# Four-layer sequence model on one core: shared expert mixtures for chunks 2 and 3 (latent) and for chunks 0 and 1 (distance), and new written orders for every engine

## The reference, cut to what matters

```python
# L0 (stage B): gates from the top two logits with a jitter mask, experts of width 256
h = silu(x @ w_gate[e].T) * (x @ w_up[e].T);  out += dense_w[:, e:e+1] * (h @ w_down[e].T)
# L1 "latent" (stage D2): softmax router, top 2, width 128, and one expert shared by all tokens
rw = softmax(nx @ Wr.T + expert_bias); topw, topi = top_k(rw, 2); topw = softmax(topw)
moe_out = swiglu(nx, sW1, sW2, sW3) + sum over the two experts of topw * swiglu_e(nx)
# L3 "distance" (stage H): the two nearest centroids, weights from a softmax over the two
#   distances, experts of width 342 with biases, gated by silu
```

## Time and profile before

| | us |
|---|---|
| runs | 1157.9, 1161.93, 1163.76 (median 1161.93) |
| profiled execution | 1159.38 |
| its span, first to last instruction | 1157.4 |
| PE busy | 920.3 |
| DVE busy | 727.3 |
| ACT busy | 609.2, of it 171.9 in 134 table loads |
| POOL busy | 403.8 |

### The profile page before, as it was taken

How to read it: one execution, slowest core, us unless ns; L and a number is a source line. 1 busy time by engine, 2 the same in 40 slices (tenths; PEclk the granted TensorE clock), 3 DMA queues, 4 the chain that set the end, 5 groups by cost and what they waited for, 6 DMA issues and landing times.

```text
span 1157.4 us, 19160 instructions
## 1 busy us (share of the span) xinstructions
PE 920.3 (80%) x5985; PEld 646.6 (56%) x5996; DVE 727.3 (63%) x2359; ACT 609.2 (53%) x1168; POOL 403.8 (35%) x443
## 2 busy tenths in 40 slices
PE   0286677995868877999958989999999989897791
PEld 0176656784647734654635645444446657687681
DVE  7684346383564776367658587876686766675442
ACT  0033255575435647687557644856567745544240
POOL 2435263535563662323324221430202203405413
PEclk9988789997869878999979999999999999988885
DMA  8246555644224103100132000000023435547771
GB/s 304 83 141 200 158 157 171 192 121 131 79 67 112 33 21 87 50 19 8 52 98 60 23 17 1 1 1 1 27 88 96 126 104 158 157 133 233 221 214 42
DMA packets 134516, 115.48 MB, mean 100 GB/s; under 512 B 11401, under 2 KB 130193, under 8 KB 134129
## 3 DMA queue, kind: packets, MB, share of 16 engines
q1 hardware_dynamic: 124704, 95.24, 28.3%
q0 software_dynamic: 6144, 12.60, 3.7%
q10 hardware_dynamic: 3568, 6.43, 1.6%
HBM read 95.08 MB, written 21.11 MB: 100 GB/s over the span
## 4 chain that ended last, share of the span: by engine, by line
PE 52%; ACT 14%; DVE 12%; issue 7%; another core or an unknown queue 5%; DMA 4%; POOL 4%; SPq 1%; POOLq 0%; ACTq 0%; DVEq 0%
PE bank L979 10%; PE bank L655 10%; PE bank L1002 5%; PE bank L597 5%; ACT L2098 5%; PE bank L701 4%; PE bank L740 2%; PE bank L604 2%; DMA att<-in_stage 2%; ACT att L2187 2%; PE bank L969 1%; PE bank L670 1%; PE bank L760 1%; PE bank L586 1%
## 5 line engine op out<-in xcount | busy, mean ns | idle before, releaser
L655 PE MATMUL bank<-xt_group,w_gu 128*128 128x128 f32 (+1 forms) x1440 | 210.2, 294 | 19.9 <-ACT hid L2136 5.7
L655 PEld LDWEIGHTS bank<-xt_group,w_gu 128*128 128x128 f32 (+1 forms) x1440 | 189.2, 200 | 36.1 <-issue 12.1
L2098 ACT ACT_TABLE_LOAD x134 | 171.9, 1283 | 36.6 <-PE bank L1002 17.2
L979 PE MATMUL bank<-picked,w_dyn 128*128 128x512 f32 x320 | 147.5, 612 | 0.7 <-DVE picked L1860 0.7
L701 PE MATMUL bank<-w_dn,hid 128*128 128x128 f32 (+1 forms) x720 | 115.2, 296 | 23.8 <-DVE hid L1493 16.8
L701 PEld LDWEIGHTS bank<-w_dn,hid 128*128 128x128 f32 (+1 forms) x720 | 99.9, 206 | 34.7 <-DVE hid L1493 19.7
L2540 POOL TENSOR_SCALAR rstd<-mv 128x4 f32<-128x4 f32 x32 | 6.6, 206 | 317.0 <-DVE mv L1305 316.3
L979 PEld LDWEIGHTS bank<-picked,w_dyn 128*128 128x128 f32 x320 | 60.5, 196 | 77.4 <-issue 75.7
L2580 POOL DMA_INDIRECT x_slots<-x,pos x64 | 62.8, 982 | 101.1 <-DVE pos L1445 84.3
L2660 POOL TENSOR_TENSOR att<-att,lsm 128x512 f32<-128x512 f32 x64 | 67.4, 1068 | 88.0 <-DVE lsm L1725 63.9
L2136 ACT ACTIVATE hid<-bank,early 114x128 f32<-114x128 f32 x180 | 52.7, 366 | 62.2 <-PE bank L655 40.6
(11 more groups left out here) (342 smaller groups left out, 1844.3 us busy)
## 6 DMA issues: line engine op xcount, KB each, us to landing
w_gu<-in_ffn SPq DMA_DIRECT2D x60, 342.0 KB
w_gu<-in_ffn SPq DMA_DIRECT2D x60, 256.0 KB
x_group<-x_slots SPq DMA_DIRECT2D x60, 192.0 KB
y_slots<-early SPq DMA_DIRECT2D x60, 192.0 KB
w_dn<-in_ffn SPq DMA_DIRECT2D x60, 192.0 KB
w_dn<-in_ffn SPq DMA_DIRECT2D x60, 128.0 KB
w_gu<-in_ffn SPq DMA_DIRECT2D x60, 128.0 KB
w_dn<-in_ffn SPq DMA_DIRECT2D x60, 64.0 KB
```

What stands on the lines that cost most here:

```text
L655: last = nc.tensor.matmul(bk[0:rows, o:o + 128], w_gate_up(k, st, j, half, f), xt_group[:, group_slot(k, st, g), c:c + 128], start=True, s ...
L979: last = nc.tensor.matmul(bk[:], part("dyn", "ex_w2")[:, h * 384 + at:h * 384 + at + 128], picked[:, 2 * h + t - 1, :], start=False, stop= ...
L2098: A.preload_act_table_set(name)
```

## The change

**Shared mixtures.** `SHARERS` puts chunks 2 and 3 into one D2 mixture and chunks 0 and 1 into one H mixture. The later chunk is the carrier: its blocks hold both chunks' assignments, 2048/128 + 7 = 23 blocks in 8 groups (seven of 3 and one of 2), where the two mixtures had 2 x 15 blocks in 2 x 5 groups. All of B, D2 of chunks 0 and 1, and H of chunks 2 and 3 stay alone with 15. The other chunk (2 in D2, 0 in H) has no turns, units, loads or stores of its own; it routes, scatters into the carrier's slots, waits for the carrier's last stores, gathers and combines.

**Counts.** Each sharer's counts wait for both chunks' one-hots and add the partner's totals: 1 more f32 matmul of 8 columns for the carrier, 5 for the other. `place` compares against 8 limits instead of 4. `name_blocks` works on 23 blocks and waits for the partner's counts; the biases are built in parts of at most 16 blocks.

**Set-up.** The slot arrays have 1 + 23 x 128 rows in place of 1 + 15 x 128, and the copies that fill `x_slots` grow with them. `stats` has two rotating rows in place of one per chunk.

The diff, cut:

```diff
-NB, GROUP = 15, 3
-GROUPS = NB // GROUP
-SLOTS = NB * 128
+GROUP = 3
+SHARERS = {"B": ((0,), (1,), (2,), (3,)), "D2": ((0,), (1,), (2, 3)), "H": ((0, 1), (2,), (3,))}
+def sharers(k, st):
+    return next(set_ for set_ in SHARERS[st] if k in set_)
+def carrier(k, st):
+    return sharers(k, st)[-1]
+def n_blocks(k, st):
+    return 8 * len(sharers(k, st)) + 7
+def n_groups(k, st):
+    return -(-n_blocks(k, st) // GROUP)
+MOST = max(n_blocks(set_[-1], st) for st in SHARERS for set_ in SHARERS[st])
+SLOTS = MOST * 128
...
-    "mix": ((0, "B"), (1, "B"), (2, "B"), (3, "B"), (0, "D2"), (1, "D2"), (2, "D2"), (3, "D2"), (0, "H"), (1, "H"),
-            (2, "H"), (3, "H")),
+    "mix": ((0, "B"), (1, "B"), (2, "B"), (3, "B"), (0, "D2"), (1, "D2"), (3, "D2"), (1, "H"), (2, "H"), (3, "H")),
...
@@ counts (PE)
-                pe.wait_ge(T.placed.s, T.placed.at(k, st, "counted"))
+                for q in sharers(k, st):
+                    pe.wait_ge(S[q].placed.s, S[q].placed.at(q, st, "counted"))
                 nc.tensor.matmul(bk[:, 0:40], part("const", "ones"), routing(s)[:, 40:80], start=True, stop=False)
+                for q in sharers(k, st):
+                    if q != k:
+                        for c in range(0, 40 if q > k else 8, 8):
+                            nc.tensor.matmul(bk[:, c:c + 8], part("const", "ones"), routing(q)[:, 40:48],
+                                             start=False, stop=False)
...
@@ mixture_steps (PE, ACT, DVE; SP alike)
+                if (k, st) not in MIXES:
+                    return
-                for what, n in mixture_order(st):
+                for what, n in mixture_order(k, st):
...
@@ set-up on ACT's queue
             for n in range(2):
-                act.dma_start(x_slots[n], x_in.rearrange("g d b t -> (g d b t)")[0:(1 + SLOTS) * D].rearrange(
-                    "(r d) -> r d", d=D)).then_inc(slots_set, 16)
+                for lo in range(0, 1 + SLOTS, SEQ * BATCH):
+                    hi = min(lo + SEQ * BATCH, 1 + SLOTS)
+                    act.dma_start(x_slots[n][lo:hi, :], x_in.rearrange("g d b t -> (g d b t)")[
+                        0:(hi - lo) * D].rearrange("(r d) -> r d", d=D)).then_inc(slots_set, 16)
...
@@ gather (POOL)
-                for g in (GROUPS - 2, GROUPS - 1):
-                    pool.wait_ge(*group_landing(y_stored, k, st, g))
+                c = carrier(k, st)
+                for g in (n_groups(c, st) - 2, n_groups(c, st) - 1):
+                    pool.wait_ge(*group_landing(y_stored, c, st, g))
+                if c != k and st == "D2":
+                    pool.wait_ge(T.filled, T.full(k, "D2", "up", "sh1"))
+                if c != k and st == "H":
+                    pool.wait_ge(T.filled, T.full(k, "H", "b2"))
...
@@ load_slots (SP)
                 if g == 0:
-                    sp.wait_ge(T.scattered, 128 * (list(MIX).index(st) + 1))
+                    for q in sharers(k, st):
+                        sp.wait_ge(S[q].scattered, 128 * (list(MIX).index(st) + 1))
```

More of the change, by code:

```diff
@@ L179, in mixture_order, with load_order @@
             order.append(("down", u - lag))
-    return order + [("down", u) for u in list(units_of(st))[-lag:]]
-def load_order(st):
-    at = {what: i for i, what in enumerate(mixture_order(st))}
-    gu, dn = GU_ITEMS[st], DN_ITEMS[st]
+    return order + [("down", u) for u in list(units_of(k, st))[-lag:]]
+def load_order(k, st):
+    at = {what: i for i, what in enumerate(mixture_order(k, st))}
+    gu, dn = items(k, st, PER_GU), items(k, st, PER_DN)
     loads = []
@@ L191, in load_order, with items @@
         loads.append((-10 + i if i < RING_W else at["down", unit_of(st, dn[i - RING_W][-1])], ("dn", i)))
-    for g in range(GROUPS):
+    for g in range(n_groups(k, st)):
         loads.append((-20 + g if g < 2 else at["turn", g - 2] + 0.5, ("xg", g)))
-        loads.append((at["down", unit_of(st, GROUP * g + GROUP - 1)] + 3.5, ("y", g)))
+        loads.append((at["down", last_unit(k, st, g)] + 3.5, ("y", g)))
     return [what for _, what in sorted(loads)]
-def items(per):
-    return [range(i, min(i + per, NB)) for i in range(0, NB, per)]
-GU_ITEMS = {"B": items(1), "D2": items(2), "H": items(1)}
-DN_ITEMS = {"B": items(1), "D2": items(3), "H": items(1)}
+PER_GU = {"B": 1, "D2": 2, "H": 1}
+PER_DN = {"B": 1, "D2": 3, "H": 1}
+def items(k, st, per):
+    n = n_blocks(k, st)
+    return [range(i, min(i + per[st], n)) for i in range(0, n, per[st])]
 class Signal:
@@ L376, in build @@
         dyn = sb("dyn", [128, 16, TOK])
-        early = sb("early", [128, 1026])
+        H_USERS = [q for q, u in MIXES if u == "H"]
+        h_most = [max([n_blocks(q, "H") for q in H_USERS[i::2]]) for i in range(2)]
+        early = sb("early", [128, max(1026, 768 + 6 * sum(h_most))])
         turn = early[:, 0:514].rearrange("p (c n) -> p c n", c=2)
@@ L424, in landing @@
             n = loads.index((k, st, i))
-            return sems[n % RING_W], 16 * sum(len(sizes[loads[m][1]][loads[m][2]]) for m in range(n % RING_W, n + 1, RING_W))
+            return sems[n % RING_W], 16 * sum(len(items(loads[m][0], loads[m][1], sizes)[loads[m][2]]) for m in range(n % RING_W, n + 1, RING_W))
         def gu_landing(k, st, j):
-            return landing(GU_LOADS, GU_ITEMS, gu_landed, k, st, j // len(GU_ITEMS[st][0]))
+            return landing(GU_LOADS, PER_GU, gu_landed, k, st, j // PER_GU[st])
         def dn_landing(k, st, j):
-            return landing(DN_LOADS, DN_ITEMS, dn_landed, k, st, j // len(DN_ITEMS[st][0]))
+            return landing(DN_LOADS, PER_DN, dn_landed, k, st, j // PER_DN[st])
         def group_landing(sems, k, st, g):
@@ L447, in w_down @@
             nf, rows = MIX[st]
-            per = len(DN_ITEMS[st][0])
+            per = PER_DN[st]
             at = (j % per + f) * 128
@@ L473, in bias_of @@
         def bias_of(k, j, half):
-            return bias_x[:, [q for q, u in MIXES if u == "H"].index(k) % 2, j, half, :]
+            return bias_x[H_USERS.index(k) % 2][:, j, half, :]
         def second(s, t):
@@ L667, in mixture_steps @@
                         pe.wait_ge(*group_landing(x_landed, k, st, n))
-                        for i in range(GROUP):
+                        for i in range(len(group_blocks(k, st, n))):
                             c = slice(128 * i, 128 * i + 128)
@@ L1450, in name_blocks @@
                 T = S[s]
+                NB = n_blocks(k, st)
+                for q in sharers(k, st):
+                    if q != k:
+                        dve.wait_ge(S[q].filled, S[q].full(q, st, "counts"))
                 upto = sm(s, S_P, 16)[:, 8:16]
@@ L1479, in mixture_steps @@
                 T = S[s]
-                for u in units_of(st):
+                if (k, st) not in MIXES:
+                    return
+                for u in units_of(k, st):
                     h = hid_unit(k, st, u)
```

263 lines of the change are left out of this document (144 added, 119 removed).

## The result

| | before | after |
|---|---|---|
| median of the runs, us | 1160.58 (6 runs) | 1179.23 (6 runs, 1173.32 to 1183.39) |
| ratio, 95% interval | | 1.0154 [1.0124, 1.0185] |
| profiled execution, its span | 1159.38, 1157.4 | 1173.32, 1171.5 |
| PE, DVE, ACT busy | 920.3, 727.3, 609.2 | 911.1, 715.0, 573.7 |
| mean granted clock | 0.907 | 0.891 |

The account below looks back on a forecast made before the run. PE was taken to bound the middle stretches, so PE time saved is nearly span saved. Terms summed to -10 us: 1149 from the profiled 1159.4, or 1152 in the medians' scale; 8-in-10 range 1133 to 1173.

Parts of the forecast that it names:

- PE's work removed: Seven blocks each of D2 and H go, 27.7 us; added count matmuls take 2.7; net -25 us.
- the join 3D2 to 2E: PE idles 12 us at 2E's transposes behind 16 gathers and a combine, 1F loses 1 more: +13 us.
- 3D2's xt: It follows its attention's projection by only 4 us of products and needs about 7: +3 us (0 to 5).
- 3D2's scatters and counts: 3D2's turn0 waits for two scatters, but PE has other steps to cover it: 0 (to 5) us.
- clock dips: A long PE idle is followed by the lower clock level; one such dip more: +3 us (0 to 7).
- waits that go: `oht`: 1F's `oht` wait of 11.8 us is partly filled by 3D2's steps: -4 us (0 to -8).
- waits that go: turns: Two turns of 2D2 and 3D2 among F, which waited 2.3 and 2.6 us, no longer wait: -5 us.
- F's starts: 2F and 3F start later with less filler; 19 us needed from logits to `oht`: +5 us together (0 to 10).
- tables: ACT loads 20 tables fewer, 25.7 us of loads, part of it counted at `oht`: -6 us (0 to -17).
- H's half, all terms: Sharing the H mixture of chunks 0 and 1, all its terms of the forecast together: -16 us.
- Rival B: The join is late: at 2E's transposes PE idles 39 us in place of 13, slower at 1178 us; chance 0.18.
- D2's part: Sharing the D2 mixture of chunks 2 and 3, its terms of the forecast together: +6 us.

Follow-up runs that it names:

- h_same: The same kernel as `h_only`, run on a chip without the stalls, against the kernel before there: 1079.59 us, ratio 0.9832.
- after_join: Kernel after, with 2D2's combine moved behind 1F's first end step and 2E's transposes behind two hidden products of 1F: 1173.57 us, ratio 1.0152 to the kernel before.
- h_only: Kernel before with only the H mixture of chunks 0 and 1 shared, D2 left as before, on a chip with stalls: 1151.9 us, ratio 0.9917.

## Why the prediction was wrong

By its own steps, in us.

| step | forecast | shown |
|---|---|---|
| PE's work removed | -25 | -30.9 + 3.3 in its own groups; of it -9.2 left in PE's busy time |
| the join 3D2 to 2E | +13 | 12.7 + 0.8 of idle, on both kinds of chip |
| 3D2's xt | +3 | 6.0, at 1E's queries just ahead of it, for the `att` buffers |
| 3D2's scatters and counts | 0 | 3.4, at 2D2's counts |
| clock dips | +3 | about +10 (half of 20.2 us more at the lower level), where no stall is |
| waits that go: `oht` | -4 | the 11.8 was a stall; without it 0.8, so nothing to win |
| waits that go: turns | -5 | all turns waited 20.5 us before, 15.8 after |
| F's starts | +5 | from the end of the logits to `oht` 8.2 in `h_same`, not 19; no idle stands there after |
| tables | -6 | 20 loads fewer, 171.9 to 146.3 us; no gain found on the path |
| set-up | +1 | 0: DVE's cast of the staging tile starts at 25.0 before, at 23.7 after |
| H's half, all terms | -16 | without stalls -17.5 alone and -13.9 on top of D2's; with them -9.7 alone |
| more and longer runs of DMAs | not in it | about +12 (the loss is 18.6 with stalls, 6.5 without); pauses took some 10 back |

The right parts: the blocks saved, H's half where no stall is, and the join, at its place, of its size (27.6 us from the last down product to 2E's transposes, forecast 26.5) and with the releaser named. Rival B put the loss at the join and gave it from 36 us of that length on; it was as long as forecast, and B fell although its sign came true. Filling the join (`after_join`) gave nothing, since 1F's own chain stood behind it. Of the signs, two held (`oht` under 9 us, 114 table loads) beside the join's, and three did not: PE was busy 911 us and not 895, idle in the F stretch was 49 and not 40, and from 3H's counts to the end it took 107.8 us in place of 101.7, which were to stay within 3. The idle at 2E (12.7 us against a limit of 25) and the idle before 261 us (2.6 more against 4) stood within what would have called the prediction wrong, so these two conditions missed the loss.

Two steps failed. The first is a term at nothing: I had counted POOL's indirect DMAs as POOL's own time, beside everything else, and the sum holds nothing for what other engines lose beside them. The new order makes POOL's DMAs of two stages stand side by side more often (3D2's scatter behind 2D2's, a gather behind 3H's scatter). By the difference between the two kinds of chip that is about 12 of the 18.6 us; it is an estimate, for the chips are compared and not the runs alone. The same mistake is in the reading of 1F's `oht`. I took its wait for the length of F's chain, charged F's starts by its 19 us and credited its loss. It stood beside a run of 16 indirect DMAs (565 to 585), and on a chip without the stall it is not there. These two terms, +5 and -4, nearly cancel, so they did little to the number. The profile of before had a sign that I did not follow: 5% of the chain under "another core or an unknown queue", on one core with no other at work. It lies in twelve pieces, each beside POOL's indirect DMAs or within 3 us behind them, 7 us of it just ahead of `oht`.

The second is D2's part without any stall, forecast +6 and measured +20. One clock dip more was forecast at 3 us. What came is a stretch of 460 us with fewer blocks to fill it, where PE idles in more places and works 20 us more at the lower level; 1E's queries wait 6.0 us where 3 were given, and 2D2's counts 3.4 where none were. The two traces add up: -6.6 of work, +13.5 of idle and about +10 of clock make 17 us, and 15.8 were measured between them. No run gave back the clock alone, so the idle is shown, the 10 of clock is the price of what the records say, and how the two hang together stays open, as do the 5 to 8 us by which the medians show D2 dearer than these two traces do.

H's half was right without stalls since it lies where PE is near full and has no such join: in `h_same` the stretch from 790 to 1060 us is 95% busy. On the first kind of chip `h_only` won 9.7 us of it; the run of 16 that its order makes, a gather behind 3H's scatter (1045 to 1065), stands in the table above with 13.5 us.

The version to keep is `h_only`: it beats both kernels on either kind of chip, 0.9917 and 0.9832.

## What to carry to other kernels

Ask of a long wait in the profile whether it is the length of its chain: look at what POOL was issuing just then, and whether other engines, SP among them, stand for the same microseconds. If they do, the wait belongs to no step, and an order that moves the steps wins nothing there and may make it longer. The surest sight of it here was the same kernel traced on two chips and laid side by side: where the lag grows is where the loss is. Before two stages' mixtures are joined, count what they filled: 8 us of removed blocks were worth less than their place between two serial chains.
